# A row sort on one Trainium2 core: the key becomes the fifth word of each element, and GpSimd makes the upper five words of a third of the pairs

## The reference, cut to what matters

```python
idx_h = argsort(xh, axis=-2); xs = take_along_axis(xh, idx_h)      # half of the channels, by columns
idx_w = argsort(xs, axis=-1); xs = take_along_axis(xs, idx_w)      # then by rows
q = conv1x1(concat(xs, rest)); cat = three depthwise convs of q     # 3x3, 5x5, 7x7
q1, k1, q2, k2, v = split(conv1x1(cat) + bias, 5)                   # 32 channels each
idx = argsort(v, over all 56*56 positions)                          # the row sort
out1 = attention(gather(q1), gather(k1), sorted v, boxed)
out2 = attention(gather(q2), gather(k2), sorted v, interleaved)
out = conv1x1(scatter back(out1) * scatter back(out2)), then idx_w and idx_h undone
```

## Time and profile before

| | us |
|---|---|
| median of 3 runs | 15,069.19 |
| lowest and highest | 15,061.56 and 15,069.54 |
| the profiled execution | 15,071.54 |
| its span, first to last instruction | 15,070.0 |
| VectorE busy | 13,765.0 |
| GpSimd busy | 6,003.7 |
| ScalarE busy | 7,124.7 |

### The profile page before, as it was taken

The page is one execution under the profiler, slowest core; times in us unless marked ns, Lnnn a source line. Parts: engine busy times, 40 slices in busy tenths (PEclk is TensorE's granted clock), DMA queues, the critical chain, the costliest instruction groups (busy, mean ns, idle before and its releaser), DMA issues. The chain is left out here.

```text
span 15070.0 us, 121660 instructions
## 1 busy us (share of the span) xinstructions
PE 6719.5 (45%) x42188; PEld 2750.0 (18%) x42188; DVE 13765.0 (91%) x8241; ACT 7124.7 (47%) x6595; POOL 6003.7 (40%) x4372
## 2 busy tenths in 40 slices
PE   4777746480026525625714813833832015433310
PEld 2443422120012112211211201211211002111100
DVE  4777778899999999999999999999999999989978
ACT  0000013355565575565565566566566555444443
POOL 0000000066666666666666666666666640000000
PEclk8888878795558757857956956966866557666655
DMA  1455543210001001000100100100100001221232
GB/s 39 117 136 127 126 111 77 58 37 12 12 12 35 27 11 36 26 12 31 31 12 30 32 12 25 37 12 13 44 17 12 33 30 51 86 66 55 77 76 66
DMA packets 343162, 699.24 MB, mean 46 GB/s; under 512 B 71581, under 2 KB 275582, under 8 KB 331702
## 3 DMA queue, kind: packets, MB, share of 16 engines
q1 hardware_dynamic: 337398, 675.91, 16.6%
q10 hardware_dynamic: 5120, 15.26, 0.5%
HBM read 480.98 MB, written 209.95 MB: 46 GB/s over the span
## 5 line engine op out<-in xcount | busy, mean ns | idle before, releaser
L1197 DVE COPY_PREDICATED arena<-psum,arena 128x4096 f32<-128x4096 uint32 (+26 forms) x1456 | 4009.7, 2771 | 46.3 <-ACT psum L1157 45.9
L1204 DVE COPY_PREDICATED arena<-psum,arena 128x4096 f32<-128x4096 uint32 (+26 forms) x1456 | 3971.4, 2744 | 42.0
L1023 PE MATMUL psum<-arena,wt 128*32 128x448 f32 x31360 | 3217.1, 572 | 1248.2 <-DMA arena<-xpad 697.1
L1122 POOL TENSOR_TENSOR arena<-arena 128x1024 int32<-128x1024 int32 (+26 forms) x1456 | 2077.8, 1433 | 3063.7 <-DVE arena L1189 3060.3
L1108 POOL TENSOR_TENSOR arena<-arena 128x1024 bf16<-128x1024 f32 (+26 forms) x1456 | 1975.4, 1363 | 3223.7 <-SPq L267 3021.4
L1145 ACT ACTIVATE arena<-arena 128x4096 f32<-128x4096 f32 (+26 forms) x1456 | 3071.5, 2126 | 70.6 <-DVE arena L1204 37.9
L1165 ACT ACTIVATE masks<-psum 128x512 fp8e4<-128x512 f32 (+27 forms) x1256 | 923.1, 736 | 3566.7 <-DVE arena L1204 3565.5
L1114 POOL TENSOR_TENSOR arena<-arena 128x1024 int32<-128x1024 int32 (+26 forms) x1456 | 2005.7, 1384 | 0.0
L1023 PEld LDWEIGHTS psum<-arena,wt 128*32 128x32 f32 x31360 | 1038.2, 115 | 3429.7 <-issue 2321.6
L1413 PE MATMUL psum<-ident,arena 128*112 128x128 f32 x896 | 197.1, 385 | 2441.6 <-ACT arena L1332 1880.7
L1189 DVE TENSOR_TENSOR arena<-arena 128x1024 f32<-128x1024 f32 (+26 forms) x1456 | 1164.2, 813 | 99.7 <-POOL arena L1114 99.7
(11 more groups left out here) (132 smaller groups left out, 7662.0 us busy)
## 6 DMA issues: line engine op xcount, KB each, us to landing
arena<-xpad SPq DMA_DIRECT2D x896, 108.5 KB, 2.3
arena<-simd SPq DMA_DIRECT2D x416, 210.0 KB, 4.3
arena<-simd SPq DMA_DIRECT2D x416, 196.0 KB, 4.2
xpad<-arena SPq DMA_DIRECT2D x8, 1924.0 KB, 8.0
arena<-in_x SPq DMA_DIRECT2D x8, 1568.0 KB, 7.7
x3d<-arena SPq DMA_DIRECT2D x8, 1568.0 KB, 5.2
prodd<-arena SPq DMA_DIRECT2D x8, 1568.0 KB, 5.1
arena<-prodd SPq DMA_DIRECT2D x8, 1568.0 KB, 13.5
```

What stands on the lines that cost most here:

```text
L1023: last = nc.tensor.matmul(psum[C * b:C * b + C, n % C_BANKS, 0:CROWS * W], wt[:, g, C * w:C * w + C], cx[i % 2][b][:, y0:y0 + CROWS, x0:x0 ...
L1122: last = nc.gpsimd.tensor_tensor(hi, packed_view(stmp, here, piece, 1), lo, ALU.subtract)
L1197: last = nc.vector.copy_predicated(lo, wide_mask(q, k, piece, here), hi)
L1204: last = nc.vector.copy_predicated(hi, wide_mask(q, k, piece, here), packed_view(ptmp, here, piece, NP))
```

## The change

The key moves into the array of the travelling words: `rowp[b]` holds five words side by side for each element (word 5n + w, the key is w = 4), so neighbouring keys lie 20 bytes apart. `lower` copies all five words of every pair under the mask, and `lower_v` is gone. The pairs of each lot are cut in two by `shared_lot`: about two thirds are "kept" and one third is "given" (70,155 and 34,840 pairs of the network). For the kept ones ACT copies the five lower words aside (`keep`) and DVE makes the upper words under the mask (`upper`). For the given ones POOL adds all five words of lower and upper as 32-bit integers ahead of `lower`, and subtracts the new lower words afterwards (`sums` and `uppers`). Cutting leaves 190 pieces of kept and 195 of given pairs; `differ` and `lower` keep 182.

The order changes with it: `differ` of the next stage waits for `upper` and `uppers` (d_hi and k_up), `lower` waits for the mask words, for `keep` and for `sums`, and POOL's queue is uppers, then differ and sums of the next stage, for lot 0 and then for lot 1. The attention and the convolutions read and write the words at the new step of five; the values, which were adjacent before, are read at it as well. ACT's copy goes from 4 words of each pair to 5 words of the kept ones.

```diff
+POOL_SHARE = 0.33
...
+def shared_lot(rows):
+    total = sum(size(piece) for piece, _ in rows)
+    x, slack = total * (1 - POOL_SHARE), total / 16
+    kept, given = [], []
+    for piece, _ in rows:
+        low, high = cut_piece(piece, min(size(piece), max(0, x)), slack)
+        kept += low
+        given += high
+        x -= size(piece)
+    return kept, given
...
             def differ(q, k):
                 if q:
-                    pool.wait_ge(d_lv[k], q)
+                    pool.wait_ge(d_hi[k], q)
                     pool.wait_ge(k_up[k], q)
...
                 for piece, _, here in lot_rows(q, k):
-                    lo, hi = values(b, piece)
+                    lo, hi = keys(b, piece)
                     last = nc.gpsimd.tensor_tensor(packed_view(dbuf, here, piece, 1), lo, hi, ALU.subtract)
...
             def sums(q, k):
-                for piece, _, here in lot_rows(q, k):
-                    lo, hi = values(b, piece, i32)
-                    last = nc.gpsimd.tensor_tensor(packed_view(stmp, here, piece, 1), lo, hi, ALU.add)
+                for piece, here in shared_rows(q, k, 1):
+                    lo, hi = pair_views(rowp[b].bitcast(i32), piece, NV)
+                    last = nc.gpsimd.tensor_tensor(packed_view(ptmp.bitcast(i32), here, piece, NV), lo, hi, ALU.add)
...
             def uppers(q, k):
                 pool.wait_ge(k_sm[k], q + 1)
-                pool.wait_ge(d_lv[k], q + 1)
+                pool.wait_ge(d_lo[k], q + 1)
+                for piece, here in shared_rows(q, k, 1):
+                    lo, hi = pair_views(rowp[b].bitcast(i32), piece, NV)
+                    last = nc.gpsimd.tensor_tensor(hi, packed_view(ptmp.bitcast(i32), here, piece, NV), lo, ALU.subtract)
...
+            for k in range(2):
+                differ(0, k)
+                sums(0, k)
             for q in range(SR):
+                for k in range(2):
+                    uppers(q, k)
+                    if q + 1 < SR and q + 1 != LAST_LEVEL:
+                        differ(q + 1, k)
+                        sums(q + 1, k)
+                if q + 1 == LAST_LEVEL:
+                    for k in range(2):
+                        differ(q + 1, k)
+                        sums(q + 1, k)
...
-            def lower_v(q, k):
-                dve.wait_ge(k_sm[k], q + 1)
...
             def lower(q, k):
                 dve.wait_ge(d_cp[k], q + 1)
+                dve.wait_ge(k_sm[k], q + 1)
                 dve.wait_ge(d_mw[k], q + 1)
                 for piece, _, here in lot_rows(q, k):
-                    lo, hi = pair_views(pay[b], piece, NP)
+                    lo, hi = pair_views(rowp[b], piece, NV)
                     last = nc.vector.copy_predicated(lo, wide_mask(q, k, piece, here), hi)
...
             def upper(q, k):
-                for piece, _, here in lot_rows(q, k):
-                    hi = pair_views(pay[b], piece, NP)[1]
-                    last = nc.vector.copy_predicated(hi, wide_mask(q, k, piece, here), packed_view(ptmp, here, piece, NP))
+                for piece, here in shared_rows(q, k, 0):
+                    hi = pair_views(rowp[b], piece, NV)[1]
+                    last = nc.vector.copy_predicated(hi, wide_mask(q, k, piece, here), packed_view(ptmp, here, piece, NV))
```

More of the change, by code:

```diff
@@ L179, with cut_piece, group @@
 assert all(lot_size(q, 0) <= lot_at(q, 1) for q in range(len(ROW_LOTS)))
+POOL_SHARE = 0.33
+def cut_piece(piece, x, slack):
+    base, nb, sb, j0, ng, sg, w, d = piece
+    block, n = ng * w, size(piece)
+    for unit in (block, w, 8, 1):
+        if w % unit and unit < w:
+            continue
+        c = min(n, max(0, round(x / unit) * unit))
+        if abs(c - x) <= slack:
+            break
+    b, rest = divmod(c, block)
+    g, i = divmod(rest, w)
+    low, high = [], []
+    def group(into, lo, hi):
+        if lo < hi:
+            into.append((base + b * sb, 1, sb, j0 + g * sg + lo, 1, 0, hi - lo, d))
+    if b:
+        low.append((base, b, sb, j0, ng, sg, w, d))
+    if g:
+        low.append((base + b * sb, 1, sb, j0, g, sg, w, d))
+    group(low, 0, i)
+    if i:
+        group(high, i, w)
+    first = g + (i > 0)
+    if rest and first < ng:
+        high.append((base + b * sb, 1, sb, j0 + first * sg, ng - first, sg, w, d))
+    done = b + (rest > 0)
+    if done < nb:
+        high.append((base + done * sb, nb - done, sb, j0, ng, sg, w, d))
+    assert sum(map(size, low)) == c and sum(map(size, low + high)) == n
+    return low, high
+def shared_lot(rows):
[8 more added lines that the diff above has]
+    return kept, given
+SHARED = [[shared_lot(rows) for rows in lots] for lots in ROW_LOTS]
 for q, (first, second) in enumerate(ROW_LOTS):
+    assert all(kept and given for kept, given in SHARED[q])
     assert sum(size(x) for x, _ in first + second) == ROW_NET[q][2]
@@ L980, in word @@
         def word(b, w):
[L981 removed]
+            return rowp[b].rearrange("p (n w) -> p n w", w=NV)[:, :, w]
         c_in, c_mm, c_ev = [sem("c_in0"), sem("c_in1")], sem("c_mm"), sem("c_ev")
@@ L1036, in c_scalar @@
                 for w in range(NWD):
-                    dst = vrow[b] if w == NP else word(b, w)
+                    dst = word(b, w)
                     act.wait_ge(c_mm, n + 1)
@@ L1047, in program @@
         d_mw, d_mcp, d_cp, d_lo, d_hi = ([sem(f"d_{n}{k}") for k in range(2)] for n in ("mw", "mcp", "cp", "lo", "hi"))
-        d_lv = [sem(f"d_lv{k}") for k in range(2)]
         d_mst = [sem(f"d_mst{i}") for i in range(4)]
-        d_sems = [*k_df, *k_sm, *k_up, *d_mw, *d_mcp, *d_cp, *d_lo, *d_hi, *d_lv, *d_mst]
+        d_sems = [*k_df, *k_sm, *k_up, *d_mw, *d_mcp, *d_cp, *d_lo, *d_hi, *d_mst]
         pmask = psum[:, 4:8, :].rearrange("p k n -> p (k n)")
@@ L1058, in lot_rows, with shared_rows @@
                 here += size(piece)
+        def shared_rows(q, k, part):
+            kept, given = SHARED[q][k]
+            here = lot_at(q, k) + (sum(map(size, kept)) if part else 0)
+            for piece in (kept, given)[part]:
+                yield piece, here
+                here += size(piece)
         def word_at(q, k):
@@ L1076, in mask_runs, with keys @@
             return runs
-        def values(b, piece, dt=f32):
-            return pair_views(vrow[b].bitcast(dt), piece, 1)
+        def keys(b, piece):
+            return pair_views(word(b, NP), piece, 1)
         def d_sync(sp, t, beside, slots=SLOTS):
@@ L1173, in d_scalar @@
                         mask_copy(s - 1, k)
-                    keep_pay(s, k)
+                    keep(s, k)
                     mask_words(s, k)
@@ L1217, in d_vector @@
                 upper(s, 1)
-                for _ in range(4, slots):
+                for _ in range(3, slots):
                     next(beside, None)
@@ L1559, in program @@
         uws = [arena[:, WS_AT + N * i:WS_AT + N * (i + 1)] for i in range(2)]
-        u_late = [pay[1][:, N * w:N * (w + 1)] for w in range(NP)]
-        u_x3 = [*uws, vrow[1]]
+        u_late = [rowp[1][:, N * w:N * (w + 1)] for w in range(NP)]
+        u_x3 = [*uws, rowp[1][:, NP * N:]]
         u_pr = [utmp[:, 0:N], utmp[:, N:2 * N]]
```

70 lines of the change are left out of this document (22 added, 48 removed).

## The result

The changed kernel takes 16,961.69 us (median of 4 runs, 16,957.96 to 16,970.81) against 15,068.69 before: a ratio of 1.1258, 95% interval 1.1239 to 1.1278. The forecast was slower, 15,700 us, with a range up to 16,250. The sign was right and the size was not: +1893 us where +631 stood.

A forecast was written before the change was run, and what follows sets the result against it. The prediction took VectorE to bound the sort rounds before, and a near-level chain and GpSimd after. One round of 1228 and seven of 1248 us made 9964, 631 over 9333, so 15,069 + 631 = 15,700 us; range 14,960 to 16,250.

The forecast's parts named there:

- What bounds the kernel before: Eight sort rounds, 9333 us together: bound by VectorE, busy for 97% of them, with GpSimd busy for 64%.
- VectorE's 1043.5 us a round: VectorE's lowers (617 us) and uppers (426 us) in a sort round, without minima, where 1143 us stood.
- Differences at 3.3 ns: GpSimd's differences of keys 20 bytes apart: 3.3 ns an element, 379 us a round where 247 stood.
- The extrapolation from the split runs: GpSimd's differences: the step from runs of four to runs of two, carried on to single words, gave 3.5 ns.
- Sums and uppers at the long-run price: GpSimd's share: five words of 34,840 pairs at 2.14 ns each, 408 us a round for each step.
- The chain instead of the busiest engine: One lot's lower, upper, differences and sums run in series: 1207 us a round; stage-wise maximum with GpSimd and VectorE, 1221.
- the 17.5 us of the text: Time round the series of lower, upper, differences and sums in a stage of 1024 and 512 pairs, against 16.8 before.
- The first round, 1228 us: First sort round, without attention work: 1221 us by stage-wise maximum, plus 5 and 2 us where both lots wait.
- Attention hidden but for 10 us, with the close 20 a round: Sort rounds with attention: its VectorE work falls into idle time except 10 us; with 10 for the close, 1248 us.
- Cheap far keys: Rival: differences of far keys cost 2.14 ns as others do; 14,990 us, faster by 0.5%; chance 0.24.
- Cheap sums and uppers: Rival: GpSimd's sums and uppers also cost 1.67 ns or less; some 14,285 us; chance 0.04.
- Dearer short runs: Rival: GpSimd's sums and uppers cost half a nanosecond more in 23 short-run stages; about 16,130 us; chance 0.12.

The follow-up runs named there:

- handed12_less: Kernel before, plus GpSimd making four upper words for one pair per lot, VectorE's copies skipping 12% of pairs; rows come out unsorted: 14,660.87 us, ratio 0.9726.
- near_broad: Changed kernel with differences reading neighbouring weight words and VectorE's copies of the 23 narrow stages taken from one long run; output wrong: 15,438.31 us, ratio 1.0240.
- broad_runs: Changed kernel with VectorE's copies in the 23 stages of one- or two-element runs taking as many words from one long run; output wrong: 16,274.93 us, ratio 1.0802.
- sums_first: Changed kernel with GpSimd's sums of a lot placed ahead of its differences, same work and output: 17,355.48 us, ratio 1.1517.
- after_attn: Changed kernel with the attention's last matmuls reading contiguous words of another buffer; attention output wrong, sort untouched: 16,801.18 us, ratio 1.1146.

## Why the prediction was right in sign and wrong in size

- **What bounds the kernel before** (VectorE, 97%): right. Taking 454 us of upper copies from VectorE gained 411 (handed12_less against the kernel before, which took 15,072.05 us when timed beside it).
- **VectorE's 1043.5 us a round, "the surest term"**: this step failed. Measured: (5632.2 + 3807.4) / 8 = 1180, 13% more. The price of 1.1045 ns a word was carried from elements of four words, all on 16-byte multiples, to elements of five. For long runs it holds (near_broad: 1040 us for VectorE in the first round). In the narrow stages it doesn't: summed over the first round's timeline a word of the lower copies (fixed parts included; 617 us for 524,975 words is 1.18 ns in the forecast) took 1.90 ns in 12 stages of single elements, 1.40 in 11 of runs of two, 1.20 in runs of four and 1.19 beyond. The lowers of the larger lots came to 459.1 us (forecast 398.5), VectorE's uppers to 307.4 (274): +94 on the chain. Undone alone, in broad_runs, this price gave back 687 us, over half of the missing 1262.
- **Differences at 3.3 ns**: mis-sized, within its bounds. (4018 - 2120) / 512 = 3.71 ns, 426 us a round and not 379; on the chain 273 and not 243. The extrapolation from the split runs (3.5 ns) was closer than the value taken. The rule that the prediction weighed, half as much again (3.2 ns; the Trainium skill, GPSIMD Engine Reference, section Performance pitfalls for Q7 kernels), was further off; the runs give 73% over the 2.14 ns of before.
- **Sums and uppers at the long-run price**: right. 395 and 405 us a round against 408 each; 252.6 us of sums on the chain against 263.5.
- **The chain instead of the busiest engine**: right in the wide stages. 1146 against 1139 us with both prices undone, and sums_first shows that order decides. That a wide stage took the 17.5 us of the text is luck, as said above: it had fewer pairs and dearer words. VectorE's wait for the sums is 1230 / 8 = 154 us a round, as forecast. But GpSimd was to be busy for 95% with nearly no wait for VectorE; it is 86%, with 839 + 509 us of waits for lower and upper copies, because VectorE sets the pace in the narrow stages.
- **The first round, 1228 us**: 1353.2. Over eight rounds that is 125 x 8 = 1000 of the missing 1262 us. The chain's misses add up to 94 + 30 - 11 = 113; the rest may be the smaller lots' copies where VectorE alone is the bound, which wasn't worked out.
- **Attention hidden but for 10 us, with the close 20 a round**: this step failed too. The rounds with attention are 56 us longer than the first in the changed kernel, as the mean of seven (76 in near_broad), 36 more than forecast: about 250 us, nearly all the rest of the miss. The forecast let VectorE's attention work fall into its idle time at an unchanged length. But that work grew, from 34 us a round in the kernel before (1145.8 - 1111.6) to 62 (1228.5 - 1166.2): 22 of the 28 are the two steps that wait for GpSimd, which is now busy for 86% of the rounds. And VectorE waits longer for TensorE's matmuls, 142.7 us in all and not 72.8; the front part says that the values were adjacent before, which holds for half of these matmuls only. At most 23 us of a round are the slower matmuls (after_attn). That an attention step in VectorE's idle time also delays the next lower, since this idle time is the wait of a chain, was argued and not tried; how much of the longer steps reached the time stays open.
- **The rivals.** Cheap far keys: not so (3.71 ns). Cheap sums and uppers: not so. Dearer short runs: right as a thought and on the wrong engine. It was asked of GpSimd, where five-word runs cost nothing extra (395 us of sums a round against 408), and not of VectorE.

## What to carry to other kernels

A price per word holds for its layout, not for its length alone: when a change moves the element from 16 to 20 bytes, ask of each engine that touches it (here VectorE's copies, GpSimd's reads and TensorE's operand) for a row at that placing, and doubt first the term with no such row that looks surest. When work goes from VectorE to an idle GpSimd, look which VectorE instructions read SBUF alone (here the minima and two attention steps) and whether they lie in that idle time; it may be what keeps them short. Where a new dependence closes a ring between two engines, sum the ring stage by stage, and count what runs in its gaps as exposed until a trace shows otherwise.

## What the runs showed of the hardware

- A masked copy of 5115 words in runs of five that start off the 16-byte multiples took 9.78 us; in one long run, 6.15. Runs of four words placed so took 7.00 and 9.61 us for 4096 and 4092.
- GpSimd's difference of two operands at 20-byte steps: 3.71 ns an element, where the layouts of the kernel before cost 1.67 to 2.6.
- A matmul record of 392 moving float32 columns took 495 ns with contiguous columns, 868 at 16-byte steps, 878 at 20-byte and 1006 at 80-byte steps, all at a granted clock of 1.00.
- VectorE's minimum of two SBUF operands waits out GpSimd's running instruction and ends 0.28, 0.55 or 1.08 us behind it (256, 512, 1024 elements). In all the minima took 1164 us before, 1763 with GpSimd 92% busy, 1188 with most of the handed work taken away. An attention step with one SBUF tensor (512 elements) did the same: 1.97 us as a mean, 0.49 beside an idle GpSimd. The masked copies, with their mask in PSUM, kept their length (3999 against 4010 us).
